# Building layer 0's one-hot matrices with one narrowing AND and five constant-mask ANDs, and one lane mask on ScalarE in place of five

## The reference, cut to what matters

```
msg = relu(h[src] + e) + 1e-7          # h[src]: one row of 64 for each edge
ex = exp(m - seg_max[dst]); denom = segment_sum(ex, dst)
agg = segment_sum(msg * ex / denom, dst)
out = h + agg  ->  two dense layers with layer norms
```

## Time and profile before

| what | value |
|---|---|
| time, median of 3 runs (lowest, highest) | 3420.85 us (3414.14, 3431.11) |
| profiled execution, span | 3415.2 us |
| PE busy | 2701.8 us, 79% |
| DVE busy | 2874.3 us, 84% |
| ACT busy | 1783.1 us, 52% |
| POOL busy | 2315.3 us, 68% |

### The profile page before, as it was taken

How to read it: one execution, slowest core, us unless ns; L and a number is a source line. 1 busy time by engine, 2 the same in 40 slices (tenths; PEclk the granted TensorE clock), 3 DMA queues, 4 the chain that set the end, 5 groups by cost and what they waited for, 6 DMA issues and landing times.

```text
span 3415.2 us, 55099 instructions
## 1 busy us (share of the span) xinstructions
PE 2701.8 (79%) x21852; PEld 1362.3 (40%) x21852; DVE 2874.3 (84%) x2835; ACT 1783.1 (52%) x2240; POOL 2315.3 (68%) x2381
## 2 busy tenths in 40 slices
PE   2778877888278899988748899889938989899854
PEld 1334333333154444444333444444415444444423
DVE  6899999999857888898966888888875888888895
ACT  2777775666434454454433455544443545545554
POOL 5777776676257777777627777777735777777752
PEclk9889988999569999999858999999957999999975
DMA  5999999999838999999846999999963999999971
GB/s 148 280 281 305 303 288 257 282 285 281 237 119 266 280 305 302 302 286 288 214 120 211 294 306 297 282 299 304 285 153 127 292 286 302 304 298 303 283 188 39
DMA packets 1047906, 878.26 MB, mean 257 GB/s; under 512 B 911706, under 2 KB 937823, under 8 KB 1015840
## 3 DMA queue, kind: packets, MB, share of 16 engines
q1 hardware_dynamic: 941552, 478.76, 54.4%
q10 hardware_dynamic: 28960, 305.28, 23.7%
q0 software_dynamic: 77136, 90.71, 10.3%
HBM read 555.79 MB, written 318.70 MB: 256 GB/s over the span
## 4 chain that ended last, share of the span: by engine, by line
DVE 33%; PE 17%; SPq 15%; ACT 9%; DMA 9%; issue 9%; POOL 8%; DVEq 0%; ACTq 0%; POOLq 0%
PE X L562 14%; SPq L370 9%; POOL gath L500 8%; DVE decay L935 7%; DMA keep<-keep_dram 7%; DVE state_all L966 5%; DVE one_hot L1030 5%; SPq L360 5%; DVE rows_all L921 4%; DVE X L940 4%; DVE state_all L950 2%; ACT X L681 2%; ACT msg L679 2%; SPq L349 1%; ACT x_sb L708 1%
## 5 line engine op out<-in xcount | busy, mean ns | idle before, releaser
L500 POOL DMA_INDIRECT gath<-z_table,idx x2248 | 2193.5, 976 | 861.8 <-issue 691.1
L562 PE MATMUL X<-one_hot,z_parts 128*64 128x512 fp8e5 x11550 | 1356.4, 397 | 148.5 <-DVE one_hot L1030 124.8
L562 PEld LDWEIGHTS X<-one_hot,z_parts 128*64 128x64 bf16 x11550 | 667.9, 115 | 874.2 <-DVE one_hot L1030 163.1
L562 PE MATMUL X<-between,z_parts 128*64 128x512 fp8e5 x6750 | 764.2, 386 | 0.0
L691 ACT ACTIVATE decay<-X 128x1024 f32<-128x1024 f32 (+2 forms) x216 | 209.4, 969 | 922.0 <-DVE X L940 909.5
L562 PEld LDWEIGHTS X<-between,z_parts 128*64 128x64 bf16 x6750 | 381.0, 112 | 393.3 <-issue 74.3
L921 DVE STREAM_TRANSPOSE rows_all<-state_all 128x1024 f32<-128x1024 f32 (+3 forms) x432 | 505.9, 1171 | 18.1 <-DMA rows_table<-rows_all 10.7
L543 PE MATMUL X<-attr,enc_edge 64*64 64x512 f32 (+1 forms) x1648 | 270.0, 706 | 309.6 <-DVE state_all L966 300.2
L950 DVE TENSOR_TENSOR_SCAN state_all<-decay,state_all,X 128x1024 f32<-128x1024 f32 (+2 forms) x216 | 468.1, 2167 | 20.0 <-ACT X L696 20.0
L935 DVE TENSOR_TENSOR_SCAN decay<-X,decay 128x1023 f32<-128x1023 f32 (+2 forms) x216 | 477.2, 2209 | 7.7
L966 DVE TENSOR_TENSOR_SCAN state_all<-decay,state_all,X 128x1024 f32<-128x1024 f32 (+2 forms) x216 | 468.0, 2167 | 0.0
(11 more groups left out here) (160 smaller groups left out, 1456.3 us busy)
## 6 DMA issues: line engine op xcount, KB each, us to landing
rows_table<-rows_all SPq DMA_DIRECT2D x784, 256.0 KB
attr<-attr_t SPq DMA_DIRECT2D x196, 512.0 KB
one_hot<-one_hot_dram ACTq DMA_DIRECT2D x48, 1920.0 KB
between<-one_hot_dram ACTq DMA_DIRECT2D x45, 1920.0 KB
one_hot<-one_hot_dram ACTq DMA_DIRECT2D x48, 1280.0 KB
one_hot_dram<-one_hot SPq DMA_DIRECT2D x31, 1920.0 KB
between<-one_hot_dram ACTq DMA_DIRECT2D x45, 1280.0 KB
one_hot_dram<-one_hot SPq DMA_DIRECT2D x31, 1280.0 KB
```

The source lines that it names most:

```text
L500: pool.indirect_dma_start(out=gath[s][:, n * F:(n + 1) * F], out_offset=None, in_=z_table, in_offset=bass.IndirectOffsetOnAxis(ap=idx[:, c ...
L562: last = nc.tensor.matmul(x[h * F:(h + 1) * F, BANK:CH], z_parts[:, i * GB + k, third, :], bank[:, i, k, h * BANK:(h + 1) * BANK], start=F ...
```

## The change

ScalarE now makes one mask for a bank: 255 where the lane is the partition's own, 0 elsewhere. VectorE first ANDs a part's 2 or 3 byte rows with it (512 or 768 words) into `own_bits`, which lies in `x_sb`, waits for that, and then makes the five tiles of k of all the part's pieces with one instruction for each k: an AND of `own_bits` with a constant word held as one value on each partition (`bit_mask`). Each writes 2 or 3 runs of 256 words, 1280 words apart. `built` is raised by the last instruction of a part, by the number of its pieces, so that all pieces of a part come at once. The mask buffers' reuse is guarded by the new semaphore `narrowed`, and that of `own_bits` by `built`.

```diff
-            def spread_lanes(n, ks):
-                if ks[0] == 0:
-                    act.wait_ge(bits_landed[n % BIT_SLOTS], 16 * (n // BIT_SLOTS + 1))
-                    if n > 0:
-                        act.wait_ge(spread, GB * n)
-                    nc.scalar.activation(lane_miss, lane_bytes[n % BIT_SLOTS], ACT.Abs, bias=lane_off[:, :]).then_inc(off_lane, 1)
-                    act.wait_ge(off_lane, n + 1)
-                    if n > 1:
-                        act.wait_ge(built, (n - 1) * PIECES_1H)
-                for k in ks:
-                    nc.scalar.activation(lane_bits[n % 2][:, k * BW:(k + 1) * BW].bitcast(u8), lane_miss, ACT.Relu,
-                                         bias=bit_value[:, k:k + 1], scale=-float(4 << k)).then_inc(spread, 1)
+            def find_lanes(n):
+                act.wait_ge(bits_landed[n % BIT_SLOTS], 16 * (n // BIT_SLOTS + 1))
+                if n > 0:
+                    act.wait_ge(spread, n)
+                nc.scalar.activation(lane_miss, lane_bytes[n % BIT_SLOTS], ACT.Abs, bias=lane_off[:, :]).then_inc(off_lane, 1)
+                act.wait_ge(off_lane, n + 1)
+                if n > 1:
+                    act.wait_ge(narrowed, (n - 1) * len(PARTS))
+                nc.scalar.activation(own_lane[n % 2].bitcast(u8), lane_miss, ACT.Relu, bias=all_bits[:, :], scale=-255.0).then_inc(spread, 1)
...
-                if building:
-                    spread_lanes(n, range(0, 2))
+                if layer == 0 and n is not None:
+                    find_lanes(n)
                 exponents(layer, c)
-                if building:
-                    spread_lanes(n, range(2, GB))
...
+                p.mark(v.memset(bit_mask[:, k:k + 1], (4 << k) * 0x01010101))
...
-                for i in range(a, b):
-                    v.tensor_tensor(one_hot[:, i].rearrange("p k c -> p (k c)").bitcast(i32).rearrange("p (k c) -> p k c", k=GB),
-                                    lane_bits[n % 2].rearrange("p (k c) -> p k c", k=GB),
-                                    bits_words[n % BIT_SLOTS][:, i * BW:(i + 1) * BW].unsqueeze(1).broadcast_to([P, GB, BW]), ALU.bitwise_and)\
-                        .then_inc(built, 1)
+                m = n * len(PARTS) + part
+                if m >= len(PARTS):
+                    dve.wait_ge(built, (n - 1) * PIECES_1H + b)
+                v.tensor_tensor(own_bits[:, a:b, :], bits_words[n % BIT_SLOTS][:, a * BW:b * BW].rearrange("p (i c) -> p i c", c=BW),
+                                own_lane[n % 2].unsqueeze(1).broadcast_to([P, b - a, BW]), ALU.bitwise_and).then_inc(narrowed, 1)
+                dve.wait_ge(narrowed, m + 1)
+                for k in range(GB):
+                    last = v.tensor_scalar(one_hot[:, a:b, k, :].bitcast(i32), own_bits[:, a:b, :], bit_mask[:, k:k + 1], None,
+                                           ALU.bitwise_and)
+                last.then_inc(built, b - a)
```

More of the change, by code:

```diff
@@ L183, in gnn_kernel @@
         scale_of = sb("scale_of", [P, NT])
-        bit_value = sb("bit_value", [P, GB])
+        bit_mask = sb("bit_mask", [P, GB], i32)
+        all_bits = sb("all_bits", [P, 1])
         lane_off = sb("lane_off", [P, 1])
@@ L228, in gnn_kernel @@
         lane_bytes = [b[:, PIECES_1H * BW:(PIECES_1H + 1) * BW].bitcast(u8) for b in bits_now]
-        lane_bits = [shared[:, (PIECES_1H + 1) * BW:(PIECES_1H + 1 + GB) * BW].bitcast(i32),
-                     x_sb[:, :, :].rearrange("p t f -> p (t f)")[:, 0:GB * BW].bitcast(i32)]
-        lane_miss = shared[:, (PIECES_1H + 1 + GB) * BW:(PIECES_1H + 2 + GB) * BW].bitcast(u8)
+        lane_at = (PIECES_1H + 1) * BW
+        own_lane = [shared[:, lane_at + s * BW:lane_at + (s + 1) * BW].bitcast(i32) for s in range(2)]
+        lane_miss = shared[:, lane_at + 2 * BW:lane_at + 3 * BW].bitcast(u8)
+        own_bits = x_sb[:, :, :].rearrange("p t f -> p (t f)")[:, 0:PIECES_1H * BW].bitcast(i32).rearrange("p (i c) -> p i c", i=PIECES_1H)
         node_in = slots("node_in", 2, [P, TG, F])
@@ L293, in gnn_kernel @@
         banks_landed, bits_steps, bits_ready, bits_stored = sem("banks_landed"), sem("bits_steps"), sem("bits_ready"), sem("bits_stored")
-        bits_landed, off_lane, spread, built = sems("bits_landed", BIT_SLOTS), sem("off_lane"), sem("spread"), sem("built")
+        bits_landed, off_lane, spread, narrowed, built = sems("bits_landed", BIT_SLOTS), sem("off_lane"), sem("spread"), sem("narrowed"), sem("built")
         used, hot_stored, hot_landed = sem("used"), sems("hot_stored", len(PARTS)), [sems(f"hot_landed{s}_", len(PARTS)) for s in range(HOT_SLOTS)]
@@ L803, in _ @@
                     n = bank_built_for(c + 3)
-                    building = layer == 0 and n is not None
-                    if building:
-                        spread_lanes(n, range(0, 2))
+                    if layer == 0 and n is not None:
+                        find_lanes(n)
                     exponents(layer, c)
-                    if building:
-                        spread_lanes(n, range(2, GB))
                     if c < NCH - 1:
@@ L876, in _ @@
             for k in range(GB):
-                p.mark(v.memset(bit_value[:, k:k + 1], float(4 << k)))
+                p.mark(v.memset(bit_mask[:, k:k + 1], (4 << k) * 0x01010101))
                 p.mark(v.memset(scale_of[:, :].rearrange("p (i k) -> p i k", k=GB)[:, :, k:k + 1], PART_SCALE[k]))
+            p.mark(v.memset(all_bits[:, :], 255.0))
             p.mark(v.memset(top[1][:, :], 0.0))
@@ L1023, in build_part @@
                     dve.wait_ge(bits_landed[n % BIT_SLOTS], 16 * (n // BIT_SLOTS + 1))
-                    dve.wait_ge(spread, GB * (n + 1))
+                    dve.wait_ge(spread, n + 1)
                 if n > 0:
```

## The result

The changed kernel takes 3460.16 us (median of 5, 3450.53 to 3463.04) against 3427.45 us (median of 5, 3414.14 to 3439.53) for the kernel before: a ratio of 1.0092 with a 95% interval of 1.0075 to 1.0110, some 31 us slower. On another chip the same pair gave 1.0109 (1.0090 to 1.0127). The forecast was 3460 us. Two more runs had raised the median of the kernel before from 3420.85 to 3427.45 us, so the forecast difference of 39 us stands against a measured 32.7.

A forecast was written before the change was run, and what follows sets the result against it. VectorE was taken to bound layer 0; its building +43, delays beside GpSimd +8 and ScalarE's relief -12 sum to +39 us, so 3420.85 + 39 = 3460 us. The forecast's own range was 3435 to 3480 us, the 8-in-10 range 3400 to 3490.

The forecast's parts named there:

- What bounds: Layer 0: VectorE bounds it, busy 49.5 us of 50 from 500 us on; its only waits for ScalarE's L681 are 16.5 us.
- The two rates: VectorE's constant ANDs: part 1 at the full rate, 1018 ns each, part 0 at the half rate, 484 ns; +1.40 us a bank.
- The sum's first term: VectorE's building in layer 0: +1.40 us a bank, +43 us for 31 banks.
- equal halves: VectorE's constant ANDs: part 0's two rows can be cut in halves and get the half rate; part 1's three rows can't.
- the bound of 615 ns for part 1: VectorE's part 1 constant ANDs: the low bound, the time of each at the half rate.
- Rival A: All ten constant ANDs a bank at the half rate: -13 us, 3408 us, or 3392 us without delays beside GpSimd; chance 0.20.
- Beside GpSimd: Half-rate ANDs on VectorE are delayed while gathers are issued: five a bank at 0.05 us, +8 us (bounds 0 and 39).
- Rival C: GpSimd becomes the bound, blocked for half-rate ANDs' whole length; with all ten at half rate +73, 3494 us; chance 0.05.
- ScalarE: Four of six mask instructions a bank go, 141 us in all; 12 us of VectorE's waits come back (bounds 0 and 16.5).
- TensorE's late signal: Part 1's first piece comes 5.75 us behind the build's start, not 1.54; cost nothing, up to 15 us above.
- The sum: The whole kernel: +43 + 8 - 12 = +39 us, giving 3460 us; the forecast had chance 0.65.
- the range: The forecast's own range, 3435 to 3480 us, from bounds of -4 ScalarE, -8 and +31 GpSimd, +15 TensorE.

The follow-up runs named there:

- experiment 1: The changed kernel with the rows of `own_bits` 264 words apart in place of 256, so source and destination have equal row counts; ratio 1.0026 to the kernel before.
- experiment 2: The changed kernel with parts of 1 and 4 pieces in place of 2 and 3; timed once, 5111.03 us, where the kernel before took 4719 us.
- experiment 4: The kernel before, with ScalarE making one mask a bank, read five times by VectorE's unchanged ANDs (tiles of k not told apart); ratio 0.9978.
- experiment 5: The kernel before, with TensorE waiting for a whole part of the matrix and not for each piece; ratio 1.0035.
- experiment 8: Experiment 6 with the ANDs of experiment 3; 3415.74 us, ratio 0.9961 to the kernel before.
- experiment 6: The changed kernel with `built` raised after each constant and TensorE's matmuls in that order; 3452.74 us, ratio 1.0067 to the kernel before.
- experiment 7: The changed kernel with constants in the instruction and part 1 made as piece 2, then pieces 3 and 4, each signalled; 3415.59 us, ratio 0.9969.
- Experiment 3: Experiment 1 with the five constants in the instruction in place of values read from a tile; ratio 1.0013 to the kernel before.

## Why the prediction was right, point by point

**What bounds.** Right. Of the 16 stretches of 50 us from 100 to 900 us, VectorE is busy 49.4 us or more in 8 before and in 8 after, and never less than 45.7. (The prediction says 49.5 from 500 us on; the stretch from 500 to 550 has 47.8.) The end of layer 0 moved by 35.3 us, and the spans of the two profiles differ by 38.7.

**The two rates.** Right, and the centre of it. Part 1 was priced at 1018 ns for each AND and took 1005, part 0 at 484 and took 492; the bank at +1.40 us and came out at 5.68 + 2.79 - 7.17 = +1.30. The sum's first term, 43 us, is 40. Experiments 1 and 2 show that it is the form and not the operation: the same words at 742 ns when both sides are three rows, and 1024 words in 747 ns when four rows go out. That equal halves decide was the author's surmise, and no profile shows how an instruction goes through its rows. What the traces show is each instruction's recorded pattern and its time. In the kernel before, L890, L1000 and L887 have one flat run on both sides, [128], [248] and [808], and these took 287, 289 and 635 ns; L992 goes from [1600] to [64,25] and L1072 from [64,25] to [1600], 25 rows of 64 against one run, in 1820 and 1821 ns. The ANDs with the constant in a tile:

| experiment | words | source | destination | mean, ns |
|---|---|---|---|---|
| 2 | 256 | [256] | [256] | 366 |
| changed kernel | 512 | [512] | [256,2] | 492 |
| 1 | 512 | [256,2] | [256,2] | 493 |
| changed kernel | 768 | [768] | [256,3] | 1005 |
| 1 | 768 | [256,3] | [256,3] | 742 |
| 2 | 1024 | [1024] | [256,4] | 747 |

One run against 3 or 25 rows is slow here, and one run against 1, 2 or 4 rows is not; other counts did not run. What the prediction took too simply is the bound of 615 ns for part 1: with three rows on both sides 263 ns of the 1005 went, where 1018 - 615 = 403 had been priced. Rival A at its best would have been experiment 1, slower than before and not faster.

**Beside GpSimd.** The sign was right and the size too large: 8 us forecast. Of the 155 ANDs of 512 words 12 take 628 to 690 ns, each of them while GpSimd issues an indirect DMA; the median is 481, so the mean of 492 gives 155 x 0.011 = 1.7 us (1.2 against the priced 484). On GpSimd's side the gathers' mean fell from 1049 to 980 ns, while VectorE spends 51 us on two-input ANDs in place of 222; in experiments 4 and 5, which keep the long two-input ANDs, it is 1041 and 1043. In the kernel before, the 177 of the 532 gathers that run at the same time as an L1030 take 1250 ns in the mean and the other 355 take 949; beside the builds of the earlier trace rows two gathers, from 212.62 and from 228.94 us, take 1.94 and 1.82 us. Rival C, a block for the instruction's whole length, is refuted: over five ANDs in a row, 2.07 us, GpSimd's gathers took 1.00 and 1.19 us, and in experiment 8, where all ten ANDs of a bank are quick and the rival priced a loss of 5.9 us a bank, the gathers' mean is 977 ns. The relief of GpSimd brings nothing that shows: it waits 106.0 us for TensorE in place of 56.1.

**ScalarE.** The mechanism was right (experiment 4), the term of 12 us is 7.5 by itself.

**TensorE's late signal.** This step was wrong in part: "I cost this at nothing, since VectorE's own longer work covers it". It costs 12 us in the kernel before (experiment 5) and 5 to 14 in the changed one (experiment 6), so the longer work covers some of it and not all. The working had TensorE's slack from a place with part 1 alone, 90 matmuls in 11.58 us. Behind 150 matmuls in a row, 16.4 us at the least, there is less slack, and all five new waits of experiment 5 are there. In the changed kernel such waits come also behind 90 matmuls where these take 12.55 and 12.64 us.

**The sum.** The whole of layer 0 can be laid out as VectorE's busy time and the rest, counted from the first instruction of layer 0's own split to that of layer 1's. These stretches of the two profiles (from, to, length, then busy us of PE, PEld, DVE, ACT, POOL) are

```profile
45.90:988.30 942.40, 673.26 (x5211) 335.81 (x5215) 877.18 (x812) 623.12 (x751) 633.02 (x606) 0.85 0.91 263
...
44.50:1023.60 979.10, 663.63 (x5219) 330.75 (x5215) 916.36 (x1030) 497.66 (x628) 596.51 (x607) 0.84 0.90 253
```

before and after, and so for each kernel (experiments 6 to 8 by their profiles from the chip where the kernel before takes 3428 us):

| kernel | layer 0, us | VectorE busy | not busy |
|---|---|---|---|
| before | 942.4 | 877.18 | 65.22 |
| changed | 979.1 | 916.36 | 62.74 |
| changed, beside experiment 6 | 975.9 | 916.55 | 59.35 |
| 1, source rows apart | 944.8 | 877.15 | 67.65 |
| 3, and constants in the instruction | 937.2 | 859.14 | 78.06 |
| 4, ScalarE's relief alone | 934.9 | 876.45 | 58.45 |
| 5, late signal alone | 953.5 | 877.63 | 75.87 |
| 6, changed, early signal | 970.5 | 915.89 | 54.61 |
| 7, everything together | 928.8 | 853.90 | 74.90 |
| 8, by constant, and fast | 930.6 | 858.42 | 72.18 |

In the changed kernel VectorE's work grew by 39 us where 43 + 8 = 51 were forecast, and its idle time fell by 2.5 us where 12 were forecast: together 36.7 against 39. So the terms for building and GpSimd were 12 us too high, those for ScalarE and the signal together 9.5 us too low, and that these errors nearly cancel is luck. The relief alone takes 6.8 us of idle time and the late signal alone adds 10.7; together in one kernel they leave 2.5 us less and not 3.9 more, which is most likely the part of the late signal that VectorE's longer work covers. Experiment 3 against experiment 1 shows the limit of the other way: 18 us less work, 10 us more waiting.

One number of the range stands without a term: the bounds that the prediction names give 3460 - 4 - 8 = 3448 us at the fast side, not 3435.

## What to carry to other kernels

Before a two-input instruction is split into cheaper one-input ones, look at how each side's rows are cut: 768 words from one run into three rows took 1005 ns here, 512 into two rows 492, and 768 with three rows on both sides 742. An instruction that covers several pieces also signals later, 5.74 us behind the build's start here in place of 1.54; test that alone, by delaying only the wait in the old kernel. A relief of an engine off the bound comes back only as far as the bound engine's waits for it reach: 7.5 us of some 141 here, with 16.5 us of such waits. And when work is taken off the bound engine, look how much of it returns as its waits: here 10 us of 18 did (experiments 1 and 3).

## What the runs showed of the hardware that was not expected

Three rows of 256 words on both sides take 742 ns, and four rows of 256 take 747 ns. A constant held in a tile costs 54 ns (768 words) and 69 ns (512 words) more for each instruction than one in the instruction, 56 and 61 by the medians, even in instructions that follow each other without a wait. And on one of the chips the kernel before took 4719 us in place of 3427. In the profiles of experiments 6, 7 and 8 from that chip TensorE is idle before matmuls of L564 for 768 to 800 us, waiting for nothing that the profile shows, at a mean granted clock of 0.79 and not 0.87; why is open. The ratios of these three kernels differ by 1 part in a hundred or less from those elsewhere, but for experiment 6 that is the difference between slower (1.0067) and faster (0.9972).
